# The links of the state chain: from TensorE and ScalarE to DMA, GpSimd and VectorE

## The chip, the cores and the metric

One core of a Trainium2 chip runs one program. The metric is the device time of an execution in microseconds (us); lower is better. PE is TensorE, DVE VectorE, ACT ScalarE, POOL GpSimd, SP SyncE, which issues all DMAs here.

## What is computed

`x` is 2 x 1024 x 128 (B, T, C), float32. The network is one residual stream: an attention A (a scan over time with a decay per channel), a mixture of experts (8 experts, 128 to 512 to 128, a gate and an up projection, silu, all experts weighted), an attention B with a matrix state per head, and the same mixture of experts again. The changed part is attention B: 16 heads with an 8 x 8 state each,

```python
def step(wkv, x):
    d, a, knt, rk, vt, rt = x
    tmp = jnp.einsum('bhj,bhjk->bhk', a * knt, wkv)
    wkv = d[..., None] * wkv - knt[..., None] * tmp[:, :, None, :] + vt[..., None] * rk[:, :, None, :]
    return (wkv, jnp.einsum('bhij,bhj->bhi', wkv, rt))
```

over 1024 steps of time for each of the 2 sequences.

## The kernel before

**The state recurrence in pieces.** The 1024 steps are cut into 2 units of 512 (`UNITS`), and a unit into 64 runs of 8 steps (`NCH` = 64, `LU` = 8). A partition holds one run of one sequence (2 x 64 = 128). So the 8 steps of all runs go side by side on DVE and POOL ("steps": T1 to T4, W1 to W5, outer, readout, read), each run starting from a zero state and also building its transition, an 8 x 8 matrix per head. Then the "chain" joins the runs: the state after run c is transition(c) times the state before it plus the local end state of run c. These 64 links of unit 0 and 63 of unit 1 (`last_link`) must go one after the other. After the chain, "back" (y0 on DVE, through on POOL, y1 on DVE, then norm and an MLP) adds to each of the 8 steps what the state before the run contributes.

**A link before.** `finish` on DVE (lines 2093 and 2097) scales transitions and end states. PE transposes both (`finish`, line 1540, four calls a unit), ACT copies them (lines 1209, 1212), so that a partition is (head, row) = 128 and a column is a run. POOL (`piece`, line 1004) spreads two runs' transitions into block-diagonal 128 x 128 matrices with `head_mask`, 32 pieces a unit, in a ring of 4. PE (`link`) adds block matrix times state (128 x 8, two matmuls, one per sequence, each float32 in two passes: 4 records) to the local part that `local_part` put into the PSUM bank by a multiplication with the identity. ACT (`link`, line 1221) copies the 16 columns into `states`, and this releases the next link. At the end `starts` on PE and ACT (line 1228) turn the states back for `back`.

**The rest.** The experts run in 8 passes of 32 chunks: passes 0 to 3 for the first mixture, 4 to 7 for the second (pass q+4 needs back q). A chunk is gate and up on PE (six 512-column matmuls), silu on ACT (line 1140), the product on DVE (line 1860, "hidden"), down on PE (8 records). At the end of each of the 64 experts, `ADDS` says whether DVE adds the result (line 2159) or ACT weighs it (line 1253) and POOL adds it (line 1024). `PE_SUMS` says which sums of the steps PE makes with an identity matmul (`work`, `ident`) and which DVE.

**What orders the work.** A planner in the kernel (`schedule`, class `Plan`) makes a list of operations with planned times and predecessors, walks through it with a priority (`rank` plus `LEAD`, `WEIGHT`, `NEAR`) and writes one fixed order per engine (`ORDER`). Each engine works through its order; a wait holds everything behind it. In PE's order of before, chunks 84 to 102 of 256 stand between the links of unit 0 and chunks 154 to 171 between those of unit 1. Front 3 (the projections of the last block of attention B) waits for pass 3 and for back 1; pass 6 waits for back 2, and the transposes of its norm stand ahead of gate chunk 189. PSUM has eight banks, which the planner hands out.

## Time and profile before

| | us |
|---|---|
| median of 3 runs | 886.38 |
| lowest and highest of the 3 | 882.91 and 2961.72 |
| profiled execution, its own time | 885.59 |
| span of that execution | 883.6 |
| PE, DVE, ACT, POOL busy | 845.0, 564.9, 376.1, 370.3 |
| granted TensorE clock, mean | 0.996 |

The span is the time from the first to the last instruction in the trace; 2.0 us of the profiled execution's own time lie around it. The prediction is made against 885.6 us.

### The profile page before, as it was taken

How to read it: one execution, taken by the hardware profiler on the slowest of the kernel's cores; microseconds unless marked ns; L12 is line 12 of the kernel's file. 1: busy time of each engine (PE TensorE's matmuls, PEld its weight loads, DVE VectorE, ACT ScalarE, POOL GpSimd, SP SyncE). 2: the span in 40 equal slices, each digit the busy share in tenths (PEclk: the TensorE clock that was granted, in tenths of full speed). 3: DMA queues.
4: the chain of work that ended last, by engine and by line, in shares of the span. 5: the costliest groups of instructions: out<-in, count | busy, mean ns of one | idle time of the engine just before them, and what ended most of it. 6: DMA issues, size and time to landing. Idle time of an engine off the chain costs nothing.

```text
span 883.6 us, 14240 instructions
## 1 busy us (share of the span) xinstructions
PE 845.0 (96%) x5342; PEld 728.3 (82%) x5342; DVE 564.9 (64%) x1056; ACT 376.1 (43%) x795; POOL 370.3 (42%) x268
## 2 busy tenths in 40 slices
PE   7999999999999899999999989999999999999997
PEld 5987987888778779897786768988998788878887
DVE  6688553798648981149699987885226789353433
ACT  5253246623682233346646625333233433444332
POOL 4443210297206865445334952786543332100000
PEclk9999999999999999999999999999999999999999
DMA  9500000011001110022110111110003311000000
GB/s 285 120 1 1 1 1 1 25 48 49 24 1 49 49 48 1 1 96 96 49 49 24 48 49 49 49 49 25 13 24 120 96 28 34 1 1 8 6 1 13
DMA packets 20989, 36.03 MB, mean 41 GB/s; under 512 B 3089, under 2 KB 9913, under 8 KB 20921
## 3 DMA queue, kind: packets, MB, share of 16 engines
q1 hardware_dynamic: 20920, 35.13, 12.1%
q8 instruction: 43, 0.70, 0.3%
q14 instruction: 26, 0.21, 0.1%
HBM read 21.49 MB, written 13.63 MB: 40 GB/s over the span
## 4 chain that ended last, share of the span: by engine, by line
PE 39%; DVE 10%; POOL 2%; issue 2%; ACT 0%; DVEq 0%; POOLq 0%; ACTq 0%
PE bank L1316 38%; DVE sh_buf L1860 1%; DVE w_a L2116 1%; DVE states L2114 1%; DVE normed L1714 1%; DVE state L2013 1%; DVE work L1959 1%; POOL readout L992 1%; POOL state L984 1%; DVE bank L2010 0%; POOL work L974 0%; DVE scr L2122 0%; DVE normed L1709 0%; POOL work L966 0%; PE bank L1342 0%
## 5 line engine op out<-in xcount | busy, mean ns | idle before, releaser
L1860 DVE TENSOR_TENSOR sh_buf<-sh_buf,bank 128x512 f32<-128x512 f32 x256 | 172.2, 683 | 220.2 <-PE bank L1316 195.3
L1316 PEld LDWEIGHTS bank<-w_down,sh_buf 128*128 128x128 f32 x2048 | 266.8, 192 | 42.0 <-DVE sh_buf L1860 21.7
L1316 PE MATMUL bank<-w_down,sh_buf 128*128 128x128 f32 x2048 | 286.8, 279 | 11.8 <-DVE sh_buf L1860 11.3
L1140 ACT ACTIVATE sh_buf<-bank 128x512 f32<-128x512 f32 x256 | 152.4, 598 | 279.1 <-PE bank L1316 233.4
L1316 PE MATMUL bank<-z_hi,w_lo 128*128 128x512 f32 x512 | 226.5, 442 | 2.0 <-DVE bank L2001 1.5
L1316 PE MATMUL bank<-z_lo,w_hi 128*128 128x512 f32 x512 | 201.9, 394 | 0.0
L1316 PE MATMUL bank<-z_hi,w_hi 128*128 128x512 f32 x512 | 201.8, 394 | 0.0
L1024 POOL TENSOR_TENSOR x<-x,y_weighted 128x512 f32<-128x512 f32 x43 | 57.5, 1336 | 223.7 <-ACT y_weighted L1253 223.6
L1316 PEld LDWEIGHTS bank<-z_lo,w_hi 128*128 128x128 f32 x512 | 96.2, 188 | 22.7 <-DVE z_lo L1871 0.4
L1316 PEld LDWEIGHTS bank<-z_hi,w_lo 128*128 128x128 f32 x512 | 97.6, 191 | 14.5 <-issue 1.9
L1316 PEld LDWEIGHTS bank<-z_hi,w_hi 128*128 128x128 f32 x512 | 97.3, 190 | 10.1 <-issue 0.2
L1004 POOL TENSOR_TENSOR backs<-backs,head_mask 128x512 f32<-128x512 f32 x64 | 69.3, 1086 | 58.6 <-PE bank L1316 55.4
L1316 PEld LDWEIGHTS bank<-states,backs 128*128 128x128 f32 x508 | 71.6, 191 | 8.5 <-issue 1.9
L1316 PE MATMUL bank<-states,backs 128*128 128x8 f32 x508 | 66.4, 239 | 0.0
L1014 POOL TENSOR_TENSOR backs<-backs,w_a 128x1024 f32<-128x1024 f32 x16 | 42.7, 2682 | 54.8 <-DVE w_a L2116 42.9
L1316 PEld LDWEIGHTS bank<-work,ident 128*128 128x128 f32 x416 | 50.0, 197 | 11.8 <-DVE work L1959 8.4
L1316 PE MATMUL bank<-work,ident 128*128 128x128 f32 x416 | 52.1, 283 | 7.3 <-DVE work L1959 4.1
L1253 ACT ACTIVATE y_weighted<-bank,cw 128x128 f32<-128x128 f32 x172 | 49.4, 369 | 18.6 <-PE bank L1316 18.3
L1221 ACT ACTIVATE states<-bank 128x16 f32<-128x16 f32 x126 | 23.0, 182 | 72.5 <-PE bank L1316 72.4
L966 POOL TENSOR_TENSOR work<-quad,rkv 128x1024 f32<-128x1024 f32 x16 | 31.3, 1954 | 48.4 <-DVE quad L1935 30.8
L992 POOL TENSOR_TENSOR readout<-state,rkv 128x1024 f32<-128x1024 f32 x16 | 40.0, 2502 | 2.8 <-DVE quad L1950 2.8
L984 POOL TENSOR_TENSOR state<-state,work 128x1024 f32<-128x1024 f32 x16 | 39.0, 2435 | 0.7
(227 smaller groups left out, 955.6 us busy)
## 6 DMA issues: line engine op xcount, KB each, us to landing
trans_spill<-state SPq DMA_DIRECT2D x16, 512.0 KB, 2.6
backs<-trans_spill SPq DMA_DIRECT2D x16, 512.0 KB, 3.3
backs<-keep_spill SPq DMA_DIRECT2D x4, 1024.0 KB, 5.5
x<-in_x SPq DMA_DIRECT2D x4, 256.0 KB, 5.9
backs<-in_w_gate SPq DMA_DIRECT2D x4, 256.0 KB, 5.2
backs<-in_w_up SPq DMA_DIRECT2D x4, 256.0 KB, 5.4
keep_spill<-rkv SPq DMA_DIRECT2D x4, 256.0 KB, 2.5
keep_spill<-low SPq DMA_DIRECT2D x4, 256.0 KB, 2.6
```

What stands on the lines that cost most here:

```text
L966: pool.tensor_tensor(outer.rearrange("p (h i k) -> p h i k", h=H, i=N), vs[:, i, :].rearrange("p (h i) -> p h i", h=H).unsqueeze(3).broadc ...
L984: pool.tensor_tensor(trans, trans, prod_t, ALU.subtract).then_inc(S["trans_rdy"], 1)
L992: pool.tensor_tensor(readout[:].rearrange("p (h i k) -> p h i k", h=H, i=N), locst.rearrange("p (h i k) -> p h i k", h=H, i=N), over_i(rec ...
L1004: pool.tensor_tensor(blocks_d[:, p % RING].rearrange("p c b (h i) -> p (c b) h i", h=H), src.unsqueeze(2).broadcast_to((P, PIECE * B, H, N ...
L1014: pool.tensor_tensor(t_ring[t % 2].rearrange("p (h i j) -> p h i j", h=H, i=N), t_ring[t % 2].rearrange("p (h i j) -> p h i j", h=H, i=N), ...
L1024: pool.tensor_tensor(flat(x[:, G * j:G * j + G, :]), flat(x[:, G * j:G * j + G, :]), y_weighted[:], ALU.add).then_inc(S["x_added"], 1)
L1140: act.activation(s_buf[:, m % 2, :], bank_of("gate", m)[:], ACT.Silu).then_inc(S["silu_done"], 1)
L1221: act.activation(dst, bank_of("links", u)[:, first:first + B * N].rearrange("p (b k) -> p b k", b=B), ACT.Copy).then_inc(S["link_rdy"], 1)
L1253: ins = act.activation(y_weighted[:, i * P:(i + 1) * P], bank_of("y", eg)[:, i * P:(i + 1) * P], ACT.Identity, scale=cw[:, q % 2, i, e:e + 1])
L1316: return pe.matmul(dst, lhs, rhs, start=start, stop=stop, **kw)
L1714: return dve.tensor_tensor(normed[:, n % 2], normed[:, n % 2], per_tile(rstd[:, n % 2, :]), ALU.mult)
L1860: dve.tensor_tensor(h_buf[:, m % 4, :], s_buf[:, m % 2, :], bank_of("up", m)[:], ALU.mult).then_inc(S["h_done"], 1)
```

## The change

Transposed block matrices go. The scaled transitions are written to a DRAM buffer, `chain_spill`, by two DMAs a unit (`spill_D`, in pieces of 256 bytes), and read back by eight DMAs of 512 KB a unit (`load_D`, 8 runs each, every row repeated over the 8 partitions that need it) into three slots (`chain_t`). A link is then a product of 128 x 128 elements (`link_mul`: transition times state, on POOL or DVE by `MULS`) and a reduction of 128 x 144 to 128 x 16 on DVE (`link`) that takes in the local part, which ACT laid beside the products (`link_w`, one instruction for two links, in a ring of 6). In unit 0 POOL makes the products of links 0 to 31 and DVE those of 32 to 63; in unit 1 DVE makes those of links 48 to 55, POOL the others. PE keeps the transposes of the local part (two calls of four) and `starts`. The planner's numbers and lists change as well: `ADDS` has 26 adds on DVE for 21, `PE_SUMS` moves one used sum (T2 of step 12) from PE to DVE, `LEAD` is another list.

```diff
-PIECE = 2
-RING = 4
+AHEAD_W = 6
+PIECE = 8
+SLOT = (0, 1, 2, 0, 1, 2, 1, 2)
+OLDER = (0, 0, 0, 3, 3, 3, 2, 2)
+MULS = [[1, 1, 1, 1, 0, 0, 0, 0], [1, 1, 1, 1, 1, 1, 0, 1]]
...
-PE_SUMS = dict(T2=[1, 1, 1, 1, 1, 1, 0, 1, 0, 1, 1, 1, 1, 1, 1, 1], W2=[...])
+PE_SUMS = dict(T2=[0, 1, 1, 1, 1, 1, 0, 1, 0, 1, 1, 1, 0, 1, 1, 1], W2=[...])
...
-LEAD = dict(experts=[11.2, -87.7, -100.8, -18.6, -7.1, 1.4, -5.6, 3.6, ...], front=[-66.9, -115.2, -46.1, 54.6], steps=[25.1, 36.8, -35.8, -2.2], back=[17.3, 83.9, 4.9, 3.0], chain=[-5.6, 76.6], other=[57.7])
+LEAD = dict(experts=[9.7, 9.7, -87.7, -87.7, -88.0, -88.0, -10.3, -18.6, -22.3, -16.1, 12.1, 12.1, 11.5, 11.5, -90.5, -90.5], front=[-66.9, -115.2, 13.9, 35.9], steps=[59.1, 14.0, -29.2, -2.2], back=[-4.7, 83.9, 4.9, 15.0], chain=[74.4, 67.5], other=[57.7])
...
+            def spill_chain(u):
+                sp.wait_ge(S["fin_rdy"], 2 * u + 1)
+                for b in range(B):
+                    sp.dma_start(chain_spill[u, :, :, b, :].rearrange("h c m -> c h m"),
+                                 fin_t[b * NCH:(b + 1) * NCH, :].rearrange("c (h m) -> c h m", h=H)).then_inc(S["chain_out"], 16)
+            def load_chain(u, p):
+                sp.wait_ge(S["chain_out"], 16 * B * (u + 1))
...
+                elif p >= 3:
+                    sp.wait_ge(S["link_made"], NCH * u + PIECE * (p - OLDER[p] + 1))
+                src = chain_spill[u, :, PIECE * p:PIECE * (p + 1)].rearrange("h c b m -> h (c b m)").unsqueeze(1).broadcast_to((H, N, PIECE * B * N * N))
+                sp.dma_start(chain_t[SLOT[p]].rearrange("p (o m) -> p o m", o=1), src).then_inc(chain_in[SLOT[p]], 16)
...
-            def piece(u, p):
-                pool.tensor_tensor(blocks_d[:, p % RING]..., src..., head_mask..., ALU.mult).then_inc(S["bd_rdy"], 1)
+            def link_mul(u, c):
+                if c == 0:
+                    pool.wait_ge(S["first_rdy"], u + 1)
+                else:
+                    pool.wait_ge(S["link_rdy"], n)
...
+                pool.tensor_tensor(link_parts[:, c % AHEAD_W].rearrange("p (b i) j -> p b i j", b=B)[:, :, :, 0:N],
+                                  chain_t[SLOT[p]][:, at:at + B * N * N].rearrange("p (b i j) -> p b i j", b=B, i=N),
+                                  states[:, c].unsqueeze(2).broadcast_to((P, B, N, N)), ALU.mult).then_inc(S["link_made"], 1)
...
-            def link(u, c):
-                act.wait_ge(S["link_full"], n + 1)
-                act.activation(dst, bank_of("links", u)[:, first:first + B * N]..., ACT.Copy).then_inc(S["link_rdy"], 1)
+            def link_w(u, g):
+                if g >= AHEAD_W // 2:
+                    act.wait_ge(S["link_rdy"], NCH * u + 2 * g + 2 - AHEAD_W)
+                act.activation(link_parts[:, s:s + 2, :, N]..., local_T[:, 2 * g * B * N:(2 * g + 2) * B * N]..., ACT.Copy).then_inc(S["link_w_rdy"], 1)
...
-            def local_part(u, half):
-                mm(bank_named[name][:], ident[:], local_T[:, first:first + BT], stop=False, skip_group_check=True)
-            def link(u, c):
-                for b in range(B):
-                    ins = mm(bank_of("links", u)[...], blocks_d[...], states[:, c, b, :], start=False, skip_group_check=True)
-                ins.then_inc(S["link_full"], 1)
...
+            def link_mul(u, c):
+                dve.tensor_tensor(link_parts..., chain_t..., states..., ALU.mult).then_inc(S["link_made"], 1)
+            def link(u, c):
+                dve.wait_ge(S["link_w_rdy"], NCH // 2 * u + c // 2 + 1)
+                dve.wait_ge(S["link_made"], n + 1)
+                dst = states[:, c + 1] if c + 1 < NCH else last_state[:]
+                dve.tensor_reduce(dst.rearrange("p b j -> p (b j)"), link_parts[:, c % AHEAD_W], AX_X, ALU.add).then_inc(S["link_rdy"], 1)
```

## Rows read from the trace of the kernel before

**Rows 1.** The page: busy time and share of each engine, and instructions.
```profile
PE 845.0 (96%) x5342; PEld 728.3 (82%) x5342; DVE 564.9 (64%) x1056; ACT 376.1 (43%) x795; POOL 370.3 (42%) x268
```

**Rows 2.** Stretches: length, then busy (x count) of each engine, PEclk, DMA share, GB/s.
```profile
320.00:392.00 72.00, 71.55 (x521) 65.63 (x523) 21.48 (x38) 25.11 (x100) 38.50 (x36) 1.00 0.08 25
...
392.00:592.00 200.00, 188.80 (x1156) 157.42 (x1153) 170.38 (x274) 101.92 (x182) 111.40 (x60) 0.98 0.15 54
...
600.00:667.00 67.00, 67.00 (x487) 61.48 (x488) 20.24 (x34) 19.96 (x82) 33.40 (x30) 1.00 0.09 30
667.00:720.00 53.00, 49.74 (x313) 41.65 (x310) 40.35 (x67) 22.73 (x41) 21.13 (x12) 1.00 0.24 78
```

**Rows 3.** The chain that ended last, in order of time: start, us, what.
```profile
597.06 71.16 PE bank L1316 x519
...
715.08 0.60 PE bank L1342 x4
```

**Rows 4.** Line 1860 alone in stretches: length, DVE busy (x count), PEclk, DMA.
```profile
800.00:875.00 75.00, 22.02 (x33) 1.00 0.02 5
...
322.00:391.00 69.00, 11.00 (x16) 1.00 0.07 24
```

**Rows 5.** DVE in order of time, in unit 0's chain: start, us, instruction.
```profile
336.09 0.69 DVE L1860 TENSOR_TENSOR sh_buf<-sh_buf,bank 128x512 f32<-128x512 f32 x1 [3.42 <-PE bank L1316]
340.30 0.69 DVE L1860 TENSOR_TENSOR sh_buf<-sh_buf,bank 128x512 f32<-128x512 f32 x1 [3.53 <-PE bank L1316]
```

**Rows 6.** Groups by line: engine, operation, shapes, count, busy, mean ns, idle before.
```profile
L1004 POOL TENSOR_TENSOR backs<-backs,head_mask 128x512 f32<-128x512 f32 x64 | 69.3, 1086 | 58.6 <-PE bank L1316 55.4 <-ACT backs L1209 2.3 <-PE bank L1540 0.8
L1316 PE MATMUL bank<-states,backs 128*128 128x8 f32 x508 | 66.4, 239 | 0.0
L1221 ACT ACTIVATE states<-bank 128x16 f32<-128x16 f32 x126 | 23.0, 182 | 72.5 <-PE bank L1316 72.4
L966 POOL TENSOR_TENSOR work<-quad,rkv 128x1024 f32<-128x1024 f32 x16 | 31.3, 1954 | 48.4 <-DVE quad L1935 30.8 <-DVE state L2013 9.4 <-issue 7.8
L1959 DVE TENSOR_TENSOR work<-state,bank 128x1024 f32<-128x1024 f32 x14 | 17.0, 1216 | 1.0 <-POOL state L984 0.8
L1950 DVE TENSOR_REDUCE quad<-readout 128x128 f32<-128x1024 f32 x16 | 19.4, 1213 | 2.4 <-POOL readout L992 2.3
L1917 DVE TENSOR_REDUCE bs<-quad 128x64 f32<-128x512 f32 x4 | 2.7, 687 | 0.1
L1316 PE MATMUL bank<-backs,ident 128*128 128x512 f32 x8 | 4.3, 622 | 0.9 <-ACT backs L1212 0.9
L1316 PE MATMUL bank<-work,ident 128*128 128x128 f32 x416 | 52.1, 283 | 7.3 <-DVE work L1959 4.1 <-DVE work L1971 2.1 <-DVE sh_buf L1860 1.0
```

**Rows 7.** POOL in order of time, ahead of a wait of DVE and waiting for DVE.
```profile
305.34 2.38 POOL L992 TENSOR_TENSOR readout<-state,rkv 128x1024 f32<-128x1024 f32 x1
...
311.99 3.20 POOL L992 TENSOR_TENSOR readout<-state,rkv 128x1024 f32<-128x1024 f32 x1 [0.68 <-DVE quad L1950]
```

**Rows 8.** DVE in order of time: waiting for POOL, and what the row of POOL waited for.
```profile
307.75 0.69 DVE L2013 TENSOR_TENSOR state<-state,bank 128x512 f32<-128x512 f32 x1 [0.21 <-POOL readout L992]
...
310.61 1.21 DVE L1950 TENSOR_REDUCE quad<-readout 128x128 f32<-128x1024 f32 x1
311.74 1.21 DVE L2093 TENSOR_TENSOR backs<-state,cumdec 128x1024 f32<-128x1024 f32 x1
```

**Rows 9.** ACT in order of time: the copy of the first link of unit 0.
```profile
321.96 0.18 ACT L1221 ACTIVATE states<-bank 128x16 f32<-128x16 f32 x1 [1.13 <-PE bank L1316]
```

**Rows 10.** DMA issues: queue, count, KB each, median us from issue to landing.
```profile
trans_spill<-state SPq DMA_DIRECT2D x16, 512.0 KB, 2.6
backs<-trans_spill SPq DMA_DIRECT2D x16, 512.0 KB, 3.3
...
x<-in_x SPq DMA_DIRECT2D x4, 256.0 KB, 5.9
```

**Rows 11.** The same columns as rows 2, in a stretch of 10 us.
```profile
470.00:480.00 10.00, 8.03 (x37) 5.10 (x36) 9.20 (x16) 7.10 (x10) 3.18 (x2) 0.83 0.18 54
```

More of the change, by code:

```diff
@@ L339, in chain @@
            dve(("finish", u, 1), 2.3, on("dve", "W5", last), on("dve", "finish", u, 0), port=True)]
-    for r in range(4):
-        out += [pe(("finish_T", u, r), 0.44, on("dve", "finish", u, r // 2), *((on("pe", "finish_T", u, r - 1),) if r else ()),
+    out.append(sp(("spill_D", u), 3.2, on("dve", "finish", u, 0)))
+    for r in range(2):
+        out += [pe(("finish_T", u, r), 0.44, on("dve", "finish", u, 1), *((on("pe", "finish_T", u, r - 1),) if r else ()),
                    takes=((("fin", u, r), on("act", "finish_T", u, r)),)),
@@ L344, in chain @@
     for p in range(PIECES):
-        after = (on("act", "finish_T", u, 1), on("pe", "finish_T", u, 1 if p < RING // 2 else 3)) if p < RING else (on("pe", "link", u, PIECE * (p - RING + 1) - 1),)
-        out.append(pool(("piece", u, p), 1.07, *after, *((on("pool", "piece", u, p - 1),) if p else ()), port=True))
+        after = (on("pe", "finish_T", u, 1),) if p == 2 else (on(multiplier(u, PIECE * (p - OLDER[p])), "link_mul", u, PIECE * (p - OLDER[p] + 1) - 1),) if p >= 3 else ()
+        if p == 0 and u:
+            after += (on("dve", "back_norm", BU * u - 1),)
+        out.append(sp(("load_D", u, p), 3.6, on("sp", "spill_D", u), *after))
+    for g in range(NCH // 2):
+        after = (on("act", "link_w", u, g - 1),) if g else (on("act", "finish_T", u, 1),) + ((on("dve", "y0", BU * u - 1, G - 1),) if u else ())
+        if g >= 3:
+            after += (on("dve", "link", u, 2 * g - 5),)
+        out.append(act(("link_w", u, g), 0.24, *after))
     for c in range(NCH - (u == UNITS - 1)):
-        after = (on("act", "finish_T", u, 3),) if c == 0 else (on("act", "link", u, c - 1),)
+        after = (on("dve", "link", u, c - 1),) if c else (on("dve", "finish", u, 1),)
         if c % PIECE == 0:
-            after += (on("pool", "piece", u, c // PIECE),)
-        out += [pe(("link", u, c), 0.85 if c % (NCH // 2) == 0 else 0.47, *after, takes=((("links", u), on("act", "link", u, last_link(u))),) if c == 0 else ()),
-                act(("link", u, c), 0.19, on("pe", "link", u, c))]
+            after += (on("sp", "load_D", u, c // PIECE),)
+        out += [(pool if MULS[u][c // PIECE] else dve)(("link_mul", u, c), 0.46 if MULS[u][c // PIECE] else 0.29, *after, port=True),
+                dve(("link", u, c), 0.30, on(multiplier(u, c), "link_mul", u, c), on("act", "link_w", u, c // 2))]
     for half in range(2):
-        out += [pe(("starts", u, half), 1.01, on("act", "link", u, last_link(u)), *((on("pe", "starts", u, 0),) if half else ()),
+        out += [pe(("starts", u, half), 1.01, on("dve", "link", u, last_link(u)), *((on("pe", "starts", u, 0),) if half else ()),
                    takes=((("starts", u, half), on("act", "starts", u, half)),)),
@@ L363, in back @@
     u = j // BU
-    first = (on("pool", "piece", u, PIECES - 1), on("pe", "link", u, NCH // 2)) if j % BU == 0 else (on("dve", "back_norm", j - 1),)
+    first = (on("act", "link_w", u, NCH // 2 - 1), on(multiplier(u, NCH // 2 - 1), "link_mul", u, NCH // 2 - 1)) if j % BU == 0 else (on("dve", "back_norm", j - 1),)
     out = [sp(("load_keep", j), 7.0, on("sp", "keepA", j), on("sp", "keepB", j), *first)]
@@ L461, in lead @@
             return LEAD["back"][n[0]]
-        if kind in ("finish", "finish_T", "piece", "link", "starts"):
+        if kind in ("finish", "finish_T", "link_mul", "link_w", "link", "starts"):
             return LEAD["chain"][n[0]]
@@ L1294, in run @@
                     finish(*n)
-                elif task == "link":
-                    link(*n)
+                elif task == "link_w":
+                    link_w(*n)
                 elif task == "starts":
@@ L1668, in run @@
                     finish(*n)
-                elif task == "link":
-                    link(*n)
                 elif task == "starts":
```

147 lines of the change are left out of this document (73 added, 74 removed).

## The prediction

> **What bounds the kernel now.** I read the page first: PE is busy for 845 of 883.6 us, the next engine, DVE, for 565 [rows 1]. That makes PE look like the only bound, and the change takes work from PE. The stretches tell it apart. In unit 0's chain (320 to 392) PE is busy all the time and DVE for 21 of 72 us; in unit 1's (600 to 667) it is the same, 67 and 20 [rows 2]. The 71 us of the chain of waits from 597 to 668, where `starts` follows, are PE's queue, links and the experts' matmuls mixed [rows 3]. Between the two chains (392 to 592, back 0 and 1, front 2 and 3, the 8 steps of unit 1) PE has 189 and DVE 170 of 200 us: two engines near their limit [rows 2]. The last stretch starts with the transposes of pass 6's norm at 715 [rows 3]: pass 6 and 7, 64 chunks, can't come before back 2, which can't come before the end of chain 1.
>
> So two things set the end. One is the sum of PE's work. The other is a path: chain 0, back 0, back 1, front 3, steps 12 to 15, chain 1, back 2, then 64 chunks on PE. A saving on PE counts in full only if that path gets shorter by as much.
>
> **What leaves PE.** In a stretch with experts alone 33 chunks take 75 us, 2.27 us a chunk [rows 4]. In chain 0, with four links to a chunk, the distance from one product on DVE to the next is 340.30 - 336.09 = 4.21 us [rows 5]. A link costs PE (4.21 - 2.27) / 4 = 0.485 us, and 127 links 62 us. (By the records alone, 66.4 us busy for 508 matmuls [rows 6]; they overlap their neighbours, the distance is the better measure.) `local_part` goes: 8 records, 4.3 us at most, and its pitch is less, say 3. Half of the transposes and one sum of 26 (52.1 / 26 = 2 us [rows 6]) go: some 4. Together 69 us by the highest, 64 us as I take it. If PE were the whole story, the time would be 885.6 - 64 = 822.
>
> **What a link costs after.** A link is product, handoff, reduction, handoff, and the next waits for it, whoever makes the product. The trace has no such small operation on these engines; I bound it by straight lines through larger ones. POOL: 1.07 us (1086 ns in the mean) for 512 elements and 1.95 for 1024 gives 0.87 for 512 more, a fixed part of 0.22 and 0.43 us for 128. DVE: the product has 1.216 us at 1024 and 0.683 at 512, so 0.28 at 128; the reductions 1.213 at 1024 and 0.687 at 512, so 0.30 at 144 [rows 4 to 6]. Handoff from DVE to POOL: 311.99 - (310.61 + 1.21) = 0.17; from POOL to DVE: 307.75 - (305.34 + 2.38) = 0.03 [rows 7, 8]. DVE after itself: some 0.04. A link with POOL: 0.43 + 0.03 + 0.30 + 0.17 = 0.93; with DVE alone: 0.28 + 0.30 + 0.08 = 0.66. From below the elements alone (half the fixed parts) would give 0.7 and 0.45, from above the 512-element durations, 1.9 and 1.4.
>
> Chain 0 has 32 of each: 30 + 21 = 51 us. But DVE now stands in the chain, and a product of the experts (0.69 us) between two links delays it. PE, free of links, makes a chunk every 2.27 us. Beside a product on POOL 0.69 us of DVE costs the chain some 0.24; in DVE's half all 0.69. POOL's half becomes 30 / (1 - 0.24/2.27) = 33 us, DVE's 21 / (1 - 0.69/2.27) = 30. The other work of DVE in this stretch is 21.5 - 11 = 10 us [rows 2, 4], half on the path: 5. Sum 68 us, against 68 before (64 links at 4.21 / 4 = 1.05 is 67). Chain 1, 55 links with POOL and 8 without: (51.2 / 0.894) + (5.3 / 0.7) + 4 = 69, against 66 before. So the chains are **not** shorter: 0 and +4 us (0.03 a link rounding in). Their gain is that PE does experts beside them.
>
> Start of the chain: two DMAs out and one back in place of transposes and copies. 2.6 and 3.3 us to landing for 512 KB each [rows 10], and some 1 us to issue, 7 us in all, or 10 if the 256-byte pieces need the 5.9 us of the slowest row, against 9 us from the end of `finish` part 0 (311.74 + 1.21 [rows 8]) to the first link's copy at 321.96 [rows 9]. I cost it at 0, with -2 to +3 a unit. The Trainium skill (DMA: Bandwidth & Descriptors, "Why small descriptors are slow (HBM only)") says that small pieces pay a fixed overhead each; no row here shows what 2048 of them cost at once. The later loads wait on SP for a slot, one or two pieces of eight links (8 us each) ahead of use, against 3.3 us to land: hidden, unless SP is held by a wait in front of them. Queued behind such a wait are the keeps and spills of the steps, whose readers come later. `load_keep` now waits for the last `link_w`, some 3 us ahead of the chain's end, and `starts` covers most of its landing: 0 to 3.
>
> ACT loses 23 us of copies and wins 64 of some 0.2; POOL loses 69 us and wins 87 x 0.43 = 37 [rows 6]; both have room. DVE wins 127 x 0.30 + 40 x 0.28 + 2 and five adds at 1.1: 57 us, 622 in all, plus the waiting inside a link. In the four stretches of rows 2, 392 us together, DVE had 252; with 52 for the links, some 25 of unhidden waits for POOL and 2 for two adds it has 331. This is the new second bound: they can't get much below 360 us.
>
> **The sum.**
> Up to 320: nothing of the links; passes 0 and 1, fronts and steps as before. A lower priority of pass 2 can take some products out of DVE's way in the steps: -4 (bounds +2 and -10).
> Chain 0: 0 (-8 to +20).
> 392 to 592: in chain 0 PE now makes 69 / 2.27 = 30 chunks for 16 [rows 4], so 14 chunks, 32 us of PE and 10 of DVE, are gone from here. PE has 189 - 34 = 155, DVE 170 - 10 + 2 = 162 left. The bound is then DVE, which had 85% of the stretch, PE 94%. At 200 - 38 = 162 DVE would be never idle; at 200 nothing is won. I take nearly half, -18: 182 us with DVE at 89%.
> Chain 1: +4 (-6 to +25).
> 667 to the first chunk of pass 6: PE has nothing old left; three and a half chunks (8 us) behind the norm's transposes have been made already, against 1 us of handoffs that they covered, and back 2's small matmuls don't queue: -9 (0 to -12).
> After it: 64 chunks and back 3 as before, 0.
> 885.6 - 4 + 0 - 18 + 4 - 9 = 858.6. I say **858 us**; the profiled run stands 0.8 us under the median of the runs. Of the 64 us, 37 turn into idle time of PE, most of it in chain 1 and back 2.
>
> **The rivals.**
> *PE counts in full.* For it: 96% busy. Against it: the 64 chunks at the end and DVE's 331 us. If the stretch 392 to 592 falls to DVE's own 165 and the chains to 62, the sum is 885.6 - 4 - 6 - 35 - 4 - 12 = 825; up to 845 I count here.
> *DVE takes PE's place.* Links, products and steps share one queue in a fixed order; the chains get 4 us longer each and the middle stretch wins only what back's small matmuls did not wait, 5: 885.6 + 4 + 4 - 5 - 9 = 880. For it: DVE has 9.2 of 10 us from 470 to 480 already [rows 11]. Within 2% of before.
> *The links are slow (slower than before).* One mechanism: a link in DVE's order holds all behind it while POOL works, and the products of the experts behind it hold PE. If a link with its neighbours takes 1.6 us where I say 1.08, 127 of them cost 66 us more: 858 + 66 = 924. It decides from 0.21 us a link (27 / 127), a pitch of 1.29, on; slower by 2% from 1.43 on. For it: the upper bound of 1.9; against it: the handoffs of 0.03 and 0.17.
> *The clock.* Where PE had 8.0 of 10 us busy, the granted clock was 0.83 [rows 11], a third of the time at the lower level of 1.2 GHz; in the four stretches of rows 2 PE falls from 377 to 313 us of some 370, 85%. If they go at 0.95 in place of 0.99, PE's work there grows by 4%, 13 us, half of it on the path: 858 + 7 = 865. The Trainium skill (TensorE: Matmul & The Clock Gate, "Part 1: The HAM clock gate") says that idleness lowers the clock and activity brings it back, so it speaks against emptying PE; the row agrees with it.
>
> **How the numbers follow.** Forecast with its own range 845 to 868: 0.50. PE in full: 0.15. The clock, 862 to 870: 0.08. DVE takes PE's place, 868 to 890: 0.19. Slow links: 0.08, most of it above 886. The measurement of this kernel tells about 2% from no change, so faster means under 868.6 and slower over 904. Faster: 0.50 + 0.15 + 0.06 = 0.71; slower 0.06; same 0.23. The range, with a tenth left out on either side, is 836 to 884.
>
> **What would show it.** PE busy near 781 us, no group of `states` and `backs` on PE; the reduction at 0.30 us and POOL's product at 0.43, 127 and 87 of them; chain 0 and 1 at 65 to 72 us from first to last link; PE idle in 600 to 700 by some 30 us; the transposes of pass 6 at about 690, and 160 us from there to the end. I'm wrong if the time from first to last link is over 80 us, if the stretch between the chains isn't shorter, or if it falls under 170 us.

## The result, and the profile after

The changed kernel takes 873.5 us in the median of 4 runs (872.9 to 873.7), the kernel before 884.6 beside it (4 runs, one of them at 2961.7; later runs of it have medians of 883.8 to 885.4): a ratio of 0.987 (95% interval 0.985 to 0.989), a gain of 11 us where I said 27 and gave 836 to 884. The profiled execution took 873.58 us with a span of 871.8. Its busy times answer to [rows 1]; below them, in 40 slices of 21.8 us, are DVE's busy tenths and the clock granted to PE.

```profile
PE 794.8 (91%) x4794; PEld 675.3 (77%) x4794; DVE 617.5 (71%) x1244; ACT 351.4 (40%) x703; POOL 335.1 (38%) x284
...
DVE  6689554678638877688899888896577868644333
...
PEclk9999999989999999969999999999999999999999
```

PE lost 50 us of busy time, 38 of them became idle time (883.6 - 845.0 = 39 before, 871.8 - 794.8 = 77 after). The stretches show where: length, then PE, PEld, DVE, ACT, POOL busy, PEclk, DMA share, GB/s.

```profile
320.00:364.00 44.00, 40.30 (x228) 34.69 (x227) 30.15 (x70) 17.63 (x46) 19.91 (x35) 0.96 0.30 85
364.00:389.40 25.40, 9.82 (x57) 8.41 (x55) 20.89 (x67) 5.64 (x20) 1.26 (x1) 0.74 0.31 97
376.70:389.40 12.70, 0.00 (x2) 0.00 (x1) 10.25 (x36) 1.55 (x6) 0.00 (x0) 0.61 0.47 151
389.00:581.00 192.00, 174.45 (x1074) 145.79 (x1075) 171.37 (x284) 89.87 (x161) 110.49 (x59) 0.98 0.16 56
593.60:662.20 68.60, 65.67 (x391) 55.50 (x389) 47.30 (x120) 24.77 (x71) 33.00 (x60) 1.00 0.27 81
662.20:720.00 57.80, 48.86 (x294) 39.37 (x293) 43.15 (x73) 18.11 (x31) 18.63 (x10) 0.97 0.23 75
```

In unit 0's chain POOL's half (to 364) has PE and DVE both at work, as forecast. DVE's half (364 to 389.4) doesn't: PE works for 9.8 of 25.4 us. The stretch between the chains (389 to 581) is 192 us long, 8 less than before, with 171 us of DVE as before [rows 2]. The experts' products on DVE say why (line 1868, the 1860 of [rows 4]), in the two halves of chain 0, between the chains and in chain 1:

```profile
325.00:364.00 39.00, 11.55 (x17) 1.00 0.25 72
364.00:389.40 25.40, 0.68 (x1) 0.74 0.31 97
389.00:581.00 192.00, 31.41 (x48) 0.98 0.16 56
594.00:662.20 68.20, 19.65 (x29) 1.00 0.26 80
```

18 products stand in chain 0, one of them in DVE's half, where the trace of before had 16 in the whole chain [rows 4]. PE, in order of time around the end of that chain, stands still for 12.7 us in one piece:

```profile
376.08 0.40 PE L1354 MATMUL bank<-z_hi,w_hi 128*128 128x512 f32 x1
376.32 0.39 PE L1354 MATMUL bank<-z_lo,w_hi 128*128 128x512 f32 x1
389.40 3.69 PE L1354 MATMUL bank<-ident,states 128*64 128x128 f32 x32 [12.70 <-DVE last_state L2134]
```

DVE, in order of time, in POOL's half and in its own (a reduction and its predecessor; in brackets the idle time before):

```profile
344.77 0.30 DVE L2134 TENSOR_REDUCE states<-w_sb 128x16 f32<-128x144 f32 x1 [0.64 <-POOL w_sb L1043]
345.71 0.30 DVE L2134 TENSOR_REDUCE states<-w_sb 128x16 f32<-128x144 f32 x1 [0.64 <-POOL w_sb L1043]
...
364.37 0.29 DVE L2124 TENSOR_TENSOR w_sb<-backs,states 128x128 f32<-128x128 f32 x1
364.77 0.30 DVE L2134 TENSOR_REDUCE states<-w_sb 128x16 f32<-128x144 f32 x1
365.11 0.29 DVE L2124 TENSOR_TENSOR w_sb<-backs,states 128x128 f32<-128x128 f32 x1
365.50 0.30 DVE L2134 TENSOR_REDUCE states<-w_sb 128x16 f32<-128x144 f32 x1
```

A link with POOL has a pitch of 0.94 us and leaves DVE 0.64 of it; one with DVE alone has 0.73 and leaves nothing but handoffs of 0.04 and 0.11. The groups by line (busy, mean ns, idle before) agree, 87 and 40 products and 126 reductions (the 127th, the last of unit 0, writes `last_state` and is counted apart):

```profile
L1043 POOL TENSOR_TENSOR w_sb<-backs,states 128x128 f32<-128x128 f32 x87 | 40.7, 468 | 65.5 <-DVE states L2134 53.7 <-DMA backs<-chain_spill 11.5
L2134 DVE TENSOR_REDUCE states<-w_sb 128x16 f32<-128x144 f32 x126 | 38.1, 303 | 34.6 <-POOL w_sb L1043 28.4
L1259 ACT ACTIVATE w_sb<-backs 128x32 f32<-128x32 f32 x64 | 16.2, 261 | 55.8 <-DVE states L2134 55.5
L2124 DVE TENSOR_TENSOR w_sb<-backs,states 128x128 f32<-128x128 f32 x40 | 13.7, 342 | 1.4 <-DVE states L2134 0.2
```

The start of a chain: DMA issues and POOL's first product in order of time, for unit 1, and the medians from issue to landing.

```profile
582.79 1.33 SPq L908 DMA_DIRECT2D chain_spill<-backs  x2
587.70 1.83 SPq L921 DMA_DIRECT2D backs<-chain_spill  x3
...
593.62 0.46 POOL L1043 TENSOR_TENSOR w_sb<-backs,states 128x128 f32<-128x128 f32 x1 [9.06 <-DMA backs<-chain_spill]
...
backs<-chain_spill SPq DMA_DIRECT2D x16, 512.0 KB, 4.8
...
chain_spill<-backs SPq DMA_DIRECT2D x4, 256.0 KB, 3.9
```

From the first issue to the product are 10.8 us; from the start of `finish` part 0 to the start of the first link's last instruction (the reduction; before, ACT's copy) it is 13.0 and 13.1 us in the two units, against 10.2 and 9.1 before.

To compare kernels I cut every trace at the same marks: start of `finish` part 0 of unit 0 (F0), last link of unit 0 (K0), `finish` part 0 of unit 1 (F1), last link of unit 1 (K1), transposes of pass 6's norm (Z), end of the span. The lengths in us, each the difference of two starts in the order of time, are those of the profiled execution; the last column is the median of all runs. The two can differ: e14 was profiled at 856.3 us, the slowest of its runs, e12 at 866.5, e1 at 867.5.

| kernel | to F0 | F0-K0 | K0-F1 | F1-K1 | K1-Z | Z-end | median |
|---|---|---|---|---|---|---|---|
| before | 311.7 | 78.7 | 200.7 | 74.3 | 49.6 | 168.6 | 884.6 |
| after | 312.8 | 76.2 | 192.1 | 80.8 | 45.0 | 164.9 | 873.5 |
| e1 DVE lighter | 313.7 | 75.8 | 188.1 | 79.8 | 45.0 | 163.3 | 869.6 |
| e2 PE 9 us lighter | 312.3 | 78.1 | 189.8 | 80.4 | 45.0 | 164.9 | 873.0 |
| e15 PE lighter | 311.9 | 78.7 | 191.2 | 80.8 | 44.9 | 163.4 | 872.2 |
| e16 both lighter | 312.3 | 77.4 | 184.6 | 80.5 | 44.9 | 163.4 | 865.9 |
| e3 early load | 313.1 | 76.1 | 194.4 | 78.8 | 44.9 | 165.0 | 873.4 |
| e4 before, half a link | 312.0 | 67.3 | 199.9 | 63.3 | 49.6 | 168.6 | 862.8 |
| e9 POOL, order kept | 312.8 | 84.6 | 193.4 | 80.5 | 44.9 | 163.3 | 883.4 |
| e10 chunks moved | 312.6 | 81.4 | 194.0 | 80.6 | 44.9 | 164.9 | 880.5 |
| e11 both | 312.9 | 84.8 | 194.0 | 80.4 | 45.1 | 164.9 | 883.4 |
| e5 lower priority | 313.1 | 82.2 | 193.2 | 81.2 | 50.8 | 165.0 | 888.7 |
| e6 POOL, planned anew | 310.8 | 95.5 | 166.5 | 80.1 | 45.0 | 163.2 | 863.7 |
| e12 e6's order, DVE | 310.7 | 97.7 | 167.7 | 80.4 | 45.0 | 163.3 | 869.1 |
| e7 old lists | 308.0 | 81.6 | 199.9 | 81.9 | 49.5 | 165.7 | 888.7 |
| e8 new lists | 305.4 | 86.8 | 177.9 | 77.2 | 47.7 | 163.6 | 860.6 |
| e13 searched | 306.8 | 76.3 | 186.0 | 70.2 | 46.8 | 163.7 | 852.2 |
| e14 searched | 303.8 | 79.4 | 184.5 | 77.1 | 46.9 | 162.7 | 850.6 |

After against before: +1.1, -2.5, -8.6, +6.5, -4.6, -3.7.

### The profile page after: what moved, and what is told of

Same layout as the page of the kernel before. It is cut to its first block and busy times, and to the rows that moved or that the text cites. A ratio compares the mean times of both kernels' runs of the same rounds, so it can differ in the third digit from the quotient of the medians.

```text
span 871.8 us, 13305 instructions
## 1 busy us (share of the span) xinstructions
PE 794.8 (91%) x4794; PEld 675.3 (77%) x4794; DVE 617.5 (71%) x1244; ACT 351.4 (40%) x703; POOL 335.1 (38%) x284
## 5 line engine op out<-in xcount | busy, mean ns | idle before, releaser
L1354 PEld LDWEIGHTS bank<-w_down,sh_buf 128*128 128x128 f32 x2048 | 269.2, 194 | 66.9 <-DVE sh_buf L1868 46.8
L1354 PE MATMUL bank<-w_down,sh_buf 128*128 128x128 f32 x2048 | 281.7, 280 | 32.0 <-DVE sh_buf L1868 31.5
L1062 POOL TENSOR_TENSOR x<-x,y_weighted 128x512 f32<-128x512 f32 x38 | 50.2, 1321 | 206.5 <-ACT y_weighted L1291 206.3
L1043 POOL TENSOR_TENSOR w_sb<-backs,states 128x128 f32<-128x128 f32 x87 | 40.7, 468 | 65.5 <-DVE states L2134 53.7
L2134 DVE TENSOR_REDUCE states<-w_sb 128x16 f32<-128x144 f32 x126 | 38.1, 303 | 34.6 <-POOL w_sb L1043 28.4
L1291 ACT ACTIVATE y_weighted<-bank,cw 128x128 f32<-128x128 f32 x152 | 43.8, 368 | 14.3 <-PE bank L1354 12.4
L982 POOL TENSOR_SCALAR var_eps<-mean_var 128x4 f32<-128x4 f32 x20 | 9.9, 496 | 93.5 <-DVE mean_var L1708 93.4
L2190 DVE SCALAR_TENSOR_TENSOR x<-bank,cw,x 128x128 f32<-128x128 f32 x104 | 29.2, 343 | 17.2 <-PE bank L1354 14.3
```

Of the source, the lines that this page charges most:

```text
L1043: pool.tensor_tensor(link_parts[:, c % AHEAD_W].rearrange("p (b i) j -> p b i j", b=B)[:, :, :, 0:N], chain_t[SLOT[p]][:, at:at + B * N * ...
L1062: pool.tensor_tensor(flat(x[:, G * j:G * j + G, :]), flat(x[:, G * j:G * j + G, :]), y_weighted[:], ALU.add).then_inc(S["x_added"], 1)
L1291: ins = act.activation(y_weighted[:, i * P:(i + 1) * P], bank_of("y", eg)[:, i * P:(i + 1) * P], ACT.Identity, scale=cw[:, q % 2, i, e:e + 1])
L1354: return pe.matmul(dst, lhs, rhs, start=start, stop=stop, **kw)
L2134: dve.tensor_reduce(dst.rearrange("p b j -> p (b j)"), link_parts[:, c % AHEAD_W], AX_X, ALU.add).then_inc(S["link_rdy"], 1)
L2190: ins = dve.scalar_tensor_tensor(out=xt(j)[:, i, :], in0=bank_of("y", eg)[:, i * P:(i + 1) * P], scalar=cw[:, q % 2, i, e:e + 1], in1=xt(j ...
```

## The experiments

My theory after the result: the 12 chunks that aren't beside chain 0 are the loss, and DVE with them. Rivals: PE's sum still bounds; the start by DRAM; the order of the work. Unless said otherwise an edit is to the changed kernel, whose own median, 873.5, is what it stands against.

### What bounds the stretch between the chains (e1, e2, e15, e16)

**e1**: DVE's product takes 128 of 512 columns in 48 chunks.

```diff
+                wide = P if 96 <= m < 160 and m % FC else BT
-                dve.tensor_tensor(h_buf[:, m % 4, :], s_buf[:, m % 2, :], bank_of("up", m)[:], ALU.mult)...
+                dve.tensor_tensor(h_buf[:, m % 4, 0:wide], s_buf[:, m % 2, 0:wide], bank_of("up", m)[:, 0:wide], ALU.mult)...
```

> The changed kernel with the same orders; for 48 of the 64 chunks 96 to 159 the product of the experts on DVE covers 128 of 512 columns (the rest of those products is left out), 0.28 us in place of 0.68, so 19 us less for DVE, all between 370 and 620 us. Theory D (after the change DVE bounds the stretch between the chains): the stretch from the last link of unit 0 to part 0 of finish of unit 1, 192 us, falls by 8 to 15 us and the time by as much, to about 862. Theory P (PE still bounds it): 3 us at most, about 871. Theory R (only the way through DRAM at the start of a chain is late): no change in that stretch.

869.6 us (867.5 to 871.0): 4 us less for 12 us less of DVE in the stretch (171.5 to 159.3). That is between what the two theories gave.

**e2**: one of two matmuls of a half of "down" in the same chunks.

```diff
-                for i in range(2 * half, 2 * half + 2):
+                for i in range(2 * half, 2 * half + (1 if 96 <= m < 160 and m % FC else 2)):
```

> The changed kernel with the same orders; for the same 48 chunks PE makes two of the four down products (the others are left out), 0.43 us each, 21 us less for PE in the same stretch. Theory D: under 5 us, about 870. Theory P: 12 to 20 us, about 856. Beside the run with DVE relieved this tells which engine bounds the stretch, since both take about 20 us from one engine at the same places.

873.0 us (870.1 to 873.4): 9 us less of PE there (174.6 to 165.7) bring half a microsecond, which is not clear of the spread of the runs.

**e15**: a third of gate and up left out in these chunks.

```diff
+                if light:
+                    return mm(bank, hi, z_hi[:, q % 2, :], start=False)
```

> The changed kernel with the third of the three matmuls of gate and of up (low part of z times high part of the weights) left out in 48 chunks of passes 3 and 4, which stand mostly in the stretch between the chains: about 96 x 0.40 = 38 us of PE less there, DVE as before. If PE has no part in the bound of that stretch, nothing comes of it, as with the 9 us of e2 (872 to 874). If PE and DVE bound it in turns, 4 to 12 us (861 to 869). If PE alone did, 30 us (843).

872.2 us (871.3 to 874.4), again within the spread of the runs. 96 matmuls are left out, but PE's busy time fell by 16 us in all (794.8 to 778.9) and by 10 in the stretch, not by the 38 of the expectation. The 38 multiplied by the 0.40 us that one record lasts, and records overlap: in the rows above the one at 376.32 starts 0.24 us after the one at 376.08. By that distance 96 of them are 23 us; the profiled execution of e3, where PE has all its work, differs by 4 us from the changed kernel's (799.1), so what is left of the gap may be no more than that. The test of PE is therefore one with 10 us taken off, and not with 38.

**e16**: e15 with e1.

```diff
+                if light:
+                    return mm(bank, hi, z_hi[:, q % 2, :], start=False)
...
+                wide = P if 96 <= m < 160 and m % FC else BT
```

> e15_pe_lighter and e1_dve_light together: in the same 48 chunks 38 us less on PE and about 14 less on DVE. If each engine's own sum were the bound, it is the better of the two alone. If the two bound the stretch in turns (PE waits for a product, DVE for a chunk), the gains of the two add up or more: e1's 4 us and e15's, and over 10 us together. If the stretch hangs on neither but on the round trips of the steps, it stays within 3 us of e1's 869.6.

865.9 us (864.6 to 867.0), 7.6 less. The stretch in the traces of e15 and e16, in the same columns as above, and the longest waits of PE for DVE's products in e16 (us in total, times, longest):

```profile
389.20:581.00 191.80, 163.79 (x1004) 135.73 (x1005) 172.58 (x287) 89.03 (x161) 110.32 (x59) 0.96 0.16 57
```

```profile
389.00:575.00 186.00, 162.31 (x1012) 135.53 (x1013) 160.39 (x287) 89.58 (x162) 111.47 (x59) 0.96 0.17 61
```

```profile
PE bank L1354 <- DVE sh_buf L1871: 12.8, 8, 5.1
```

Neither engine's sum alone is the bound. 10 us off PE are worth nothing that can be told from noise, 12 us off DVE a third of that, both together 7.6 us. The 10 us that e16's expectation set for "in turns" weren't reached, nor did it stay within 3 us of e1's 869.6. In e16 PE and DVE are each idle for over 23 of 186 us, PE for 12.8 of them in 8 waits for a product of DVE. That most of the length is the order with its round trips is my reading of this; e6 and e12 below, which change the order, bear it out, but no run isolates it.

### Does the start count (e3)

The first load of a unit reads other data, so that it needn't wait for `chain_spill`.

```diff
-                sp.wait_ge(S["chain_out"], 16 * B * (u + 1))
+                if p:
+                    sp.wait_ge(S["chain_out"], 16 * B * (u + 1))
+                else:
+                    sp.wait_ge(S["fin_rdy"], 2 * u + 1)
+                    sp.wait_ge(S["spilled"], 16 * (LU * u + 1))
...
+                if p == 0:
+                    src = spill[LU * u, 0:H].unsqueeze(1).broadcast_to((H, N, PIECE * B * N * N))
```

> The changed kernel; the first of the eight loads of a chain reads an old spill of the steps and is issued ahead of the chain's spill, so the first eight links don't wait for the way through DRAM (their transitions are other data). Theory R: the first link comes some 4 to 5 us earlier in each unit, and the time falls by 6 to 9 us, to about 865. Theory D: in unit 0 the gain is lost to the products of DVE behind it, in unit 1 it is kept: 3 to 5 us, about 869.

873.4 us (868.0 to 874.1, one run of four under 873): nothing in the median. In the trace the start did get shorter, from 13.0 to 11.3 us in unit 0 and from 13.1 to 10.4 in unit 1. There POOL's first product began 6.6 us behind F1 and the first reduction 3.9 us after that: in the fixed orders ACT's copies with `link_w` (to 593.0) and a product of the experts on DVE (from 593.5) stood ahead of it. Chain 1 ended up 2 us shorter; the stretch ahead of it was 2.3 longer in this trace, and why is open. So the way by DRAM was worth 1.7 and 2.6 us of start, and other work ends almost as late.

### What a microsecond of chain is worth (e4, e9, e10, e11)

**e4** is the kernel before with one of a link's two matmuls.

```diff
-                for b in range(B):
+                for b in range(1):
```

> The kernel before, where PE makes the link of one of the two sequences only (the other's is left out): 127 links at half of 0.485 us, 31 us less for PE, and nothing put on DVE. If a microsecond of link on PE is a microsecond of the kernel (the base of the forecast), the pitch of four links and a chunk falls from 4.21 to 3.25 us, each chain by 15 us and the time by 25 to 31, to about 856. If the path has other parts that then end last, under 15.

862.8 us, 21 less than the 883.8 of before beside it. Both chains are 11 us shorter where 15 were expected, the 200 us between them stay, and no stage but the chains moved.

**e9**: the orders kept, the products of links 32 to 63 of unit 0 taken from DVE's list and put into POOL's.

```diff
+    for c in range(32, 64):
+        d.remove(("link_mul", 0, c))
+        p.insert(at + c - 32 + (c > 44), ("link_mul", 0, c))
```

> The orders of the changed kernel, kept as they are on every engine, with one thing moved: the products of links 32 to 63 of unit 0 stand on POOL (in one row, POOL's add behind the thirteenth of them) and not on DVE. A link there takes 0.94 us in place of 0.74, so the chain ends 6.4 us later, and DVE has free time of 0.64 us a link in which its order holds almost nothing. Theory O (the gain of the run with all products on POOL lies in what the orders put into that free time): 5 to 7 us slower than the changed kernel, about 879. Theory E (it lies in the engine itself, DVE being relieved): no slower, 873 or less.

883.4 us. The chain is 8.4 us longer, the end 10 later, more than either theory gave.

**e10**: the opposite cure, six chunks (99 to 104) moved ahead into DVE's half.

```diff
+    for i, g in enumerate(range(99, 105)):
+        d.remove(("hidden", g))
+        d.insert(d.index(("link", 0, 44 + 3 * i)) + 1, ("hidden", g))
```

> The orders of the changed kernel, with DVE making the products as there, and six of the experts' products (chunks 99 to 104), with the matmuls and silus that belong to them, moved ahead from behind the chain to between links 44 and 59; everything else in the same order. The chain ends 6 x 0.68 = 4.1 us later; 4.1 us of DVE and some 9 us of PE leave the stretch behind. If DVE's time alone counts, the two cancel: 872 to 876. If PE counts there: 868 or less.

880.5 us. The chain got 5 us longer, and the stretch behind it, six chunks poorer, is 194.0 us, not shorter: as built, the chunks beside the chain bought nothing behind it. PE had work in DVE's half now (21.6 of 30 us, and 4.3 us of standing still ahead of `starts` for 12.7). The half and the stretch in e10, then the first 10 us behind the chain in e10 and, below it, in the changed kernel, all in the columns of the stretches above:

```profile
364.00:394.00 30.00, 21.63 (x123) 17.83 (x121) 25.71 (x76) 9.77 (x31) 2.48 (x4) 0.93 0.27 83
394.00:588.00 194.00, 172.37 (x1017) 141.15 (x1018) 168.41 (x279) 87.06 (x154) 110.67 (x59) 0.94 0.16 55
394.00:404.00 10.00, 7.54 (x40) 5.25 (x41) 8.58 (x15) 4.39 (x6) 5.19 (x4) 0.50 0.20 68
```

```profile
389.00:399.00 10.00, 9.35 (x56) 6.88 (x57) 9.14 (x18) 6.64 (x13) 4.11 (x4) 0.79 0.26 89
```

One rival stands beside this. The granted clock of the stretch was 0.94 for 0.98, and 0.50 in its first 10 us for 0.79; 57 records fewer took only 2 us less of PE. What the six chunks would have bought at the same clock is not known.

**e11**: e9 and e10 together.

```diff
+        p.insert(at + c - 32 + (c > 44), ("link_mul", 0, c))
...
+        d.insert(d.index(("link", 0, 44 + 3 * i)) + 1, ("hidden", g))
```

> Both edits of the two runs before: products of links 32 to 63 on POOL, six chunks moved ahead, else the orders of the changed kernel. The chain ends 6.4 + 6 x 0.26 = 8 us later than in the changed kernel, 4.1 us of DVE and 9 us of PE leave the stretch behind. By DVE's time 877, by PE's 872.

883.4 us, as e9. The chunks cost nothing where POOL makes the products (F0-K0 84.8 for 84.6), and give nothing (194.0 for 193.4, at a clock of 0.94 for 0.97). The expectations of e10 and e11, 868 to 877 us, were all too low: each let either DVE's or PE's time count in the stretch.

### Which work belongs beside the chain (e6, e12, e5)

**e6**: POOL makes all products of unit 0, and the planner orders anew.

```diff
-MULS = [[1, 1, 1, 1, 0, 0, 0, 0], [1, 1, 1, 1, 1, 1, 0, 1]]
+MULS = [[1, 1, 1, 1, 1, 1, 1, 1], [1, 1, 1, 1, 1, 1, 0, 1]]
```

> The changed kernel with POOL making all 64 products of unit 0 (the part of the change about the second half undone; the planner makes new orders from there). Nine of the experts' products stand in the second half. The half costs 32 x (0.94 - 0.74) = 6 us more for the links and about 9 x 0.3 for the products. Theory H: PE makes 8 chunks more there, 18 us of PE and 5 of DVE leave the stretch behind it, and the time falls by 4 to 10 us, to about 866. Theory L: the longer chain is paid in full, 5 to 9 us slower, about 880.

863.7 us (863.1 to 866.1), 10 less than the changed kernel. Chain 0 is 19 us longer and the stretch behind it 26 shorter; with some 2 us each ahead of F0 and behind Z that makes the 10. The second half (363 to 406.3) holds 8 products of the experts, but also front 2's keys and scale (lines 1890 to 1943) and the first removals of unit 1's steps (1979, 2029); a few of its groups by line:

```profile
L2134 DVE TENSOR_REDUCE states<-w_sb 128x16 f32<-128x144 f32 x29 | 8.8, 302 | 14.4 <-POOL w_sb L1043 12.9 <-ACT w_sb L1259 1.3
L1868 DVE TENSOR_TENSOR sh_buf<-sh_buf,bank 128x512 f32<-128x512 f32 x8 | 5.3, 675 | 0.0
L2029 DVE COPY state<-work 128x1024 f32<-128x1024 f32 x1 | 2.1, 2143 | 0.0
...
L1939 DVE TENSOR_TENSOR quad<-quad,readout 128x512 f32<-128x512 f32 x1 | 0.9, 949 | 0.0
...
L1904 DVE TENSOR_TENSOR quad<-quad 128x512 f32<-128x512 f32 x1 | 0.8, 836 | 0.0
...
L1917 DVE RECIPROCAL ss<-ss 128x64 f32<-128x64 f32 x1 | 0.6, 554 | 0.0
```

and for the changed kernel's second half the groups are links and nothing else:

```profile
L2124 DVE TENSOR_TENSOR w_sb<-backs,states 128x128 f32<-128x128 f32 x32 | 10.3, 322 | 1.2 <-DVE states L2134 0.2
L2134 DVE TENSOR_REDUCE states<-w_sb 128x16 f32<-128x144 f32 x32 | 9.7, 303 | 3.2
L1868 DVE TENSOR_TENSOR sh_buf<-sh_buf,bank 128x512 f32<-128x512 f32 x1 | 0.7, 677 | 0.0
```

In the changed kernel front 2's keys, logs and scale come behind the first products of back 0 (line 1939 at 428, 39 us after the chain's end); in e6 they lie between the links of the second half (at 398, 8 us ahead of it), where POOL's links leave DVE 0.64 us each. Was it the engine or the order?

**e12**: e6's orders, and the 32 products back on DVE, each in front of its reduction.

```diff
+    for c in range(32, 64):
+        p.remove(("link_mul", 0, c))
+        d.insert(d.index(("link", 0, c)), ("link_mul", 0, c))
```

> The order of the work of e6_pool_half is kept on every engine, and only the products of links 32 to 63 of unit 0 go back from POOL to DVE, each where its reduction stands. If it is the order that made e6 faster (DVE's work of front 2 between the links of the second half, so that the stretch behind them is short), the time is e6's 863.7 within 3 us: DVE has some 32 x 0.29 = 9 us more in a second half of 43 us in which it was busy for 28.5 and each link is 0.2 us shorter. If it is the engine (DVE's own products leave no room for front 2 in the chain), the second half gets longer or the stretch behind keeps its 192 us, and the time goes back towards 873.

869.1 us (866.5 to 873.8), between both. The stretch behind the chain stays short (167.7), so its shortness is the order's; but DVE's half is no faster by its shorter links, F0-K0 is 2 us longer than e6's and F0 to F1 3.4, since every link now takes 0.73 us of DVE and not 0.30. Of the 9.9 us some 4 are the order and 5 the engine (e12's own interval is 3.5 us either way, so the split is rough).

**e5**: the planner gives the second half's links a low priority, so that other work may stand between them.

```diff
+        if kind in ("link_mul", "link") and n[0] == 0 and n[1] >= 32:
+            return -80
```

> The changed kernel with a lower priority for links 32 to 63 of unit 0 alone; the orders are those of the changed kernel up to there, and then seven of the experts' products stand between those links on DVE, where one stood. Theory H (what is lost is the half of chain 0 in which DVE makes products and sums and PE stands still for want of the experts' products; chunks made there would count): the chain gets 5 us longer (7 x 0.68), PE makes 14 us of work there, the stretch behind is 9 us or more shorter; the time falls by 4 us or more, to 869. Theory L (DVE's time is the price: every product put between links is paid for at the chain's end, and what PE has ahead is of no use): slower by 2 to 6 us, about 877.

888.7 us. The chain got 6 us longer, what was put between the links (7 products and a norm) did not shorten the stretch behind it (193.2), and the planner's later order lost 6 us more in K1-Z. A miss as a cure, and it shows that a planner that orders everything anew changes more than was asked.

### The structure and the lists (e7, e8, e13, e14)

The change came with new lists for the planner. **e7** has the new links with the old lists.

```diff
-PE_SUMS = dict(T2=[0, 1, 1, 1, 1, 1, 0, 1, 0, 1, 1, 1, 0, 1, 1, 1], ...)
+PE_SUMS = dict(T2=[1, 1, 1, 1, 1, 1, 0, 1, 0, 1, 1, 1, 1, 1, 1, 1], ...)
...
-LEAD = dict(experts=[9.7, 9.7, -87.7, ...], ...)
+LEAD = dict(experts=[11.2, -87.7, -100.8, ...], ...)
```

> The changed kernel's links with the planner's numbers and lists of the kernel before (ADDS, PE_SUMS, LEAD, WEIGHT, NEAR). If the gain of 11 us is the structure's, it stays within 3 us, about 874. If it is the new numbers', it goes, about 882.

888.7 us, a ratio to before of 1.005 (1.004 to 1.007). PE is busy for 799.0 us, 46 less than before, and the stretch between the chains is 199.9 us for 200.7: with the lists of before the new way of making links wins nothing, and of the 8.6 us that the changed kernel won in that stretch all but 0.8 came with its lists.

**e8**: lists found anew, `MULS` among them, with the planner's costs of the DRAM way set to what the profile shows.

```diff
-MULS = [[1, 1, 1, 1, 0, 0, 0, 0], [1, 1, 1, 1, 1, 1, 0, 1]]
+MULS = [[1, 1, 1, 1, 1, 0, 1, 1], [1, 0, 1, 0, 1, 0, 1, 0]]
...
-    out.append(sp(("spill_D", u), 3.2, on("dve", "finish", u, 0)))
+    out.append(sp(("spill_D", u), 5.0, on("dve", "finish", u, 0)))
```

> The changed kernel's links with other numbers for the planner (15 of 16 groups of eight links may be made by either engine, 30 adds on DVE, other priorities; the way through DRAM is counted at what it measured, 5.0 and 4.8 us). No theory of the forecast hangs on it: if the fixed orders, not an engine's work, hold the changed kernel back, other orders alone reach the 858 us of the forecast or less; if DVE's work is the bound, they stay over 868.

860.6 us (860.2 to 864.8), 13 less than the changed kernel.

**e13** and **e14**: two more sets of lists found anew.

```diff
-MULS = [[1, 1, 1, 1, 0, 0, 0, 0], [1, 1, 1, 1, 1, 1, 0, 1]]
+MULS = [[1, 1, 0, 1, 1, 0, 1, 0], [1, 0, 1, 0, 1, 0, 1, 0]]
```

> The changed kernel with the lists that steer the order found anew for its own costs (which units' links POOL makes per group of eight, the due times and priorities of the passes, the DRAM way of the states at the 5 us that the profile after shows). If the order is what is left to win, it comes out under e8's 860.6, at 845 to 858. If DVE's sum of work sets the stretch between the chains whatever the order, it comes out at 860 or above.

```diff
-MULS = [[1, 1, 1, 1, 0, 0, 0, 0], [1, 1, 1, 1, 1, 1, 0, 1]]
+MULS = [[1, 1, 1, 0, 1, 1, 0, 0], [0, 1, 0, 1, 1, 0, 1, 0]]
```

> As e13_searched_a with another set of lists, which puts one more sum on DVE and gives DVE the products of other links. The same two expectations: 845 to 858 if order is what is left, 860 or above if DVE's sum of work is the bound. A difference of over 5 us between the two would say that the result hangs on single places in the order and not on the shares of the engines.

852.2 us (851.4 to 854.5) and 850.6 (847.6 to 856.3), ratios to before of 0.965 (0.962 to 0.967) and 0.963 (0.958 to 0.967): both beat both kernels, by 32 to 34 us and by 21 to 23. No run has lists found anew for the links of before, so how much of the 32 to 34 us the new links made possible, and how much a search would have won without them, is not shown. In both sets POOL's and DVE's groups of eight links mostly take turns. e13's three stages from F0 to K1:

```profile
306.80:383.10 76.30, 68.54 (x378) 56.10 (x378) 52.82 (x143) 38.30 (x92) 27.42 (x46) 0.96 0.33 93
383.10:569.10 186.00, 161.69 (x984) 135.88 (x983) 166.65 (x259) 74.90 (x144) 111.38 (x59) 0.93 0.17 58
...
569.10:639.30 70.20, 67.60 (x408) 58.23 (x406) 57.44 (x152) 30.36 (x78) 23.15 (x37) 1.00 0.35 95
```

Chain 0 is as short as in the changed kernel and has PE at 68.5 us instead of 56.4; chain 1, with half its products on DVE instead of an eighth, is 10.6 us shorter; 6 us are won ahead of F0. DVE is busier in all than in the changed kernel (620.9 us for 617.5, 629.6 in e14), so DVE's sum was not the bound of the changed kernel.

## Why the prediction was wrong, and where it was right

**The link: right.** 0.94 us with POOL for a forecast of 0.93 and 0.73 with DVE for 0.66, where the two handoffs were 0.15 and not 0.08. The straight lines through larger operations gave 0.43, 0.28 and 0.30 where 0.47, 0.29 (as in the rows; 0.34 in the mean) and 0.30 were measured; both handoffs of a link with POOL are 0.94 - 0.47 - 0.30 = 0.17 together for a forecast of 0.20. The slow-link rival is out.

**Up to 320: -4 forecast, +1.1 measured (to F0).** The lower priority of pass 2 brought nothing. e13 and e14 show that 6 to 9 us were there, by other lists.

**Chain 0: 0 forecast, -2.5 measured**, but not by the working given. I let 68 us of chain hold 30 chunks' products; it held 18. POOL's half took 39 us with 17 products where I had 33 with some 14, DVE's half 25 with one where I had 30 with some 13. So the links themselves took 5.2 us less than before (63.2 for 68.4), and the start 2.8 more.

**392 to 592: -18 forecast, -8.6 measured. This is the step that failed.** It was "in chain 0 PE now makes 69 / 2.27 = 30 chunks for 16, so 14 chunks, 32 us of PE and 10 of DVE, are gone from here". Two things in it were wrong. First, the chunks weren't made: DVE's list in its half is product, sum, product, sum, one product of the experts in all comes in between, and PE ran dry; two chunks were gained, not 14. Second, and deeper, I let PE's and DVE's sums set the stretch. With the lists of before it stays at 200 us though PE lost its links (e7). 9 and 10 us off PE bring 0.5 and 1.3 us (e2, e15), 12 off DVE 4.0 (e1), both 7.6 (e16), where the forecast let 32 us of PE and 10 of DVE bring 18. e10 and e11 put six more chunks ahead and the stretch stayed at 194 us, at a lower clock. What does shorten it is another order, in which front 2's work on DVE stands ahead of it (e6, e12: 167 us); that it is this work and not another part of the new order was not isolated. In e6 the shorter stretch and the longer chain leave a gain of 6 us from F0 to F1. Which round trip in the steps ends last stays open.

**Chain 1: +4 forecast, +6.5 measured**, 4.0 of it at the start (13.1 for 9.1), 2.4 in the links (67.7 for 65.3). The two transfers were under-sized: 3.9 us for 256 KB in pieces of 256 bytes and 4.8 for each 512 KB read back, where I went by 2.6 and 3.3. The start was 2.8 us longer in unit 0 and 4.0 in unit 1, beyond my "-2 to +3". e3 won 1.7 and 2.6 of it back, and its median is the changed kernel's.

**667 to pass 6: -9 forecast, -8.3 measured**, -4.6 to the transposes of the norm and -3.7 behind them. The sum fits and its parts don't: I had 1 us ahead of the transposes and 8 behind them, 160 us from there to the end where 164.9 were measured. They came at 706.9, not at about 690.

**The rivals.** "PE counts in full" is out: 38 of its 50 us turned to idle time, and e2 and e15 say the same. "DVE takes PE's place" came nearest by its time (880), and its picture of one queue with a fixed order holds. In POOL's half and in chain 1 other work of DVE does hold up the links (39 us where 32 links alone are 30, 67.7 where those of chain 1 alone are some 57); in DVE's half it was the reverse, and one product stood between 32 links. The clock: it was granted at 0.976 for 0.996 in the mean; 2% of 795 us are 16 us, about as much as PE's busy time stands above my 781 (14), though no run shows the one to be the other. The stretch between the chains had the 0.98 of before; DVE's half, where PE stood still for half the time, had 0.74. One place on the path shows a price. After 12.7 us of idleness the 32 matmuls of `starts` took 3.69 us; unit 1's, with PE busy ahead of them, took 2.08. The stretches of exactly those two, unit 0's and unit 1's:

```profile
389.40:393.10 3.70, 3.69 (x32) 3.28 (x32) 2.99 (x11) 1.13 (x2) 1.69 (x2) 0.50 0.56 191
```

```profile
662.50:665.00 2.50, 2.50 (x37) 2.38 (x36) 0.00 (x0) 1.21 (x3) 0.00 (x0) 1.00 0.64 210
```

0.50 is the lower level of 1.2 GHz, and at this place it cost 1.6 us. Whether the clock cost the 7 us of the rival over the whole path was not tested; e10 is a trace in which it may count. In e13 the stretch between the chains went at 0.93 and was 6 us shorter all the same. The Trainium skill (TensorE: Matmul & The Clock Gate, "Part 1: The HAM clock gate") says that an idle TensorE is clocked down until it is active again; the two rows agree with it.

Why e4 wins 21 us and the change 11: e4 shortened both chains by 22 us and left everything else. The change took the whole of the links from PE, but kept the chains' length (by F0-K0 and F1-K1, 153 us before and 157 after). Where the orders are kept, a chain's microsecond counts in full (e4: 22 for 21, e9: 8.4 for 10, e10: 5 for 7, 2 of them lost behind it), and a microsecond of PE in the stretch between the chains almost not at all (e2, e15). Where the order changes too, a chain can be 19 us longer and the kernel 10 faster (e6).

## What to carry to other kernels

When a serial chain leaves one engine for another, the freed engine's time is not the kernel's: look at which operations stand between two links in the fixed order, and whether the path behind the chain waits for them, not at the sums. A chain's link on the busiest vector engine can be shorter and still dearer: in e12 DVE's link was 0.2 us shorter than in e6, and took 0.73 us of DVE instead of 0.30 from other work; the kernel was some 5 us slower, give or take 3.5. It depends on what stands there: in e9, with almost nothing between the links, POOL's were the dearer ones, and in e13 chain 1 with half its products on DVE was 10.6 us shorter. After such a change the order is searched anew: here that was worth twice the change itself (22 us to its 11), though the same search on the kernel before was not made.
